# DeltaNet recurrence and gated experts on one core: fused state operations, router columns in the first up product, two products on VectorE

## What is computed

```python
x = x + conv(ln_c(x))                  # conv(n) = t + o @ Wo, t the tokens of n
q, k = l2norm(silu(t @ Wq)), l2norm(silu(t @ Wk))      # 12 heads of 16
v, beta = silu(t @ Wv), sigmoid(t @ Wb)
u_t = beta_t * (v_t - S_{t-1}^T k_t)   # per image and head, S is 16 x 16
S_t = S_{t-1} + k_t u_t^T;   o_t = S_t^T q_t
t = t + ffn(ln_t(t))
probs = softmax(n @ router_w); two best of 8, scaled to sum 1 -> dense_g
routed = sum_e dense_g[e] * (silu(n @ w_gate[e]) * (n @ w_up[e])) @ w_down[e]
shared = (silu(n @ ws_gate) * (n @ ws_up)) @ ws_down
alpha = sigmoid(n @ sg_w + sg_b);   ffn = alpha * shared + (1 - alpha) * routed
```

## Time and profile before

| | us |
|---|---|
| median of 3 runs (497.37 to 498.15) | 497.47 |
| the profiled execution | 497.98 |
| its span | 496.2 |
| busy in it: DVE / PE / POOL / ACT | 428.0 / 425.9 / 414.0 / 349.7 |
| mean granted clock of TensorE | 0.934 |

### The profile page before, as it was taken

The page is one execution under the profiler, slowest core; times in us unless marked ns, Lnnn a source line. Parts: engine busy times, 40 slices in busy tenths (PEclk is TensorE's granted clock), DMA queues, the critical chain, the costliest instruction groups (busy, mean ns, idle before and its releaser), DMA issues.

```text
span 496.2 us, 10722 instructions
## 1 busy us (share of the span) xinstructions
PE 425.9 (86%) x2464; PEld 391.3 (79%) x2464; DVE 428.0 (86%) x2546; ACT 349.7 (70%) x1039; POOL 414.0 (83%) x527
## 2 busy tenths in 40 slices
PE   0344276899999999999999999999999989899996
PEld 0233144789999989899898989898988979898996
DVE  2349989999999999999999999999999999997200
ACT  2795445686878787877778686878786848385763
POOL 5288699989899999999999898998999999896341
PEclk9855555999999999999999999999999999999999
DMA  7948373543323222323233332323222323200300
GB/s 203 223 100 159 94 180 100 111 103 111 79 68 88 72 78 74 92 65 102 68 84 87 81 89 78 89 72 83 80 83 74 83 78 86 81 28 0 114 2 16
DMA packets 44752, 44.12 MB, mean 89 GB/s; under 512 B 19920, under 2 KB 36496, under 8 KB 44688
## 3 DMA queue, kind: packets, MB, share of 16 engines
q1 hardware_dynamic: 40944, 40.87, 32.3%
q10 hardware_dynamic: 3744, 2.57, 1.8%
HBM read 37.13 MB, written 6.29 MB: 87 GB/s over the span
## 4 chain that ended last, share of the span: by engine, by line
DVE 73%; PE 11%; SPq 4%; issue 3%; POOL 3%; DMA 3%; ACT 2%; DVEq 0%; ACTq 0%; POOLq 0%
DVE Pr L1301 16%; DVE u L1303 15%; DVE bank L1305 15%; DVE SH L1309 12%; PE bank L427 2%; DMA k_scratch<-khl 2%; DVE st L1041 2%; SPq L249 2%; SPq L214 1%; DVE ss L1116 1%; PE bank L412 1%; DVE mv L1042 1%; DVE otok L1148 1%; DVE loT L1084 1%; PE bank L400 1%
## 5 line engine op out<-in xcount | busy, mean ns | idle before, releaser
L931 POOL TENSOR_TENSOR hid<-sg,ug 128x192 f32<-128x192 f32 x192 | 112.3, 608 | 23.0 <-ACT ug L669 21.4
L886 POOL TENSOR_TENSOR PQ<-SH,QB 128x768 f32<-128x768 f32 x62 | 112.5, 1835 | 5.8 <-DVE SH L1309 5.8
L1301 DVE TENSOR_TENSOR Pr<-SH,bank 128x96 f32<-128x96 f32 x512 | 104.8, 245 | 4.3 <-PE bank L361 3.9
L893 POOL TENSOR_TENSOR PQ<-PQ 128x768 f32<-128x768 f32 (+2 forms) x93 | 103.3, 1111 | 6.0
L1305 DVE TENSOR_TENSOR bank<-bank,u 128x96 f32<-128x96 f32 x512 | 106.5, 252 | 0.0
L427 PE MATMUL bank<-Wd,hidT 128*128 128x192 f32 x576 | 106.4, 326 | 0.0
L1303 DVE TENSOR_REDUCE u<-Pr 128x6 f32<-128x102 f32 x512 | 105.9, 247 | 0.0
L1309 DVE TENSOR_TENSOR SH<-SH,bank 128x96 f32<-128x96 f32 x512 | 103.0, 241 | 0.0
L427 PEld LDWEIGHTS bank<-Wd,hidT 128*128 128x128 f32 x576 | 95.3, 190 | 0.0
L668 ACT ACTIVATE sg<-bank 128x192 f32<-128x192 f32 x192 | 63.0, 328 | 45.0 <-PE bank L404 25.7
L361 PE MATMUL bank<-KR,Sel 128*128 128x384 f32 x128 | 58.3, 460 | 22.0 <-DVE SH L1309 12.5
(11 more groups left out here) (150 smaller groups left out, 836.6 us busy)
## 6 DMA issues: line engine op xcount, KB each, us to landing
QB<-q_scratch SPq DMA_DIRECT2D x64, 384.0 KB
k_scratch<-khl SPq DMA_DIRECT2D x64, 48.0 KB, 1.7
KR<-k_scratch SPq DMA_DIRECT2D x32, 96.0 KB, 2.4
q_scratch<-qn SPq DMA_DIRECT2D x64, 24.0 KB, 1.6
Wd<-in_L_ffn_w_down_dram SPq DMA_DIRECT2D x4, 288.0 KB, 8.0
out_dram<-xT SPq DMA_DIRECT2D x1, 896.0 KB, 5.2
Wlo_unsplit<-in_L_ffn_w_gate_dram ACTq DMA_DIRECT2D x1, 768.0 KB, 5.6
Wlo_unsplit<-in_L_ffn_w_up_dram ACTq DMA_DIRECT2D x1, 768.0 KB, 8.8
```

The source lines that it names most:

```text
L886: tt(PQ[:, at * BR * HP:(at + n) * BR * HP].rearrange("p (i b h) d -> p i b (h d)", i=n, b=BR), SH[:, lo:lo + n].rearrange("p i b h d -> p ...
L893: chained(tt(PQ[:, :, 0:w], PQ[:, :, 0:w], PQ[:, :, w:2 * w], ALU.add))
L931: tt(hid[:, r * H:(r + 1) * H], sg[:, m % RING], ug[:, m % RING], ALU.mult).then_inc(s_hid, 1)
L1301: v = each(lambda br: count(tt(Pr[:, br, i, :, 0:D], prev[:, br], KB[:, br], ALU.mult)), Sb)
```

## The change

1. In chunks 1 to 15, 17 of the 64 operations (`WHOLE`) are issued as one instruction over both halves, 192 columns; chunk 0 stays as it was. 128 instructions become 111.
2. The 9 logit columns, padded to R = 10, stand in front of unit 0's weights, are split like them, and come out of unit 0's five products, now 394 columns. `Fa_logits`, its weights and the two copies to h2T go. The maximum and the exponentials read unit 0's bank and wait for it. The router's weights are loaded in nine transfers instead of four, ahead of the up weights in SP's queue. The projection of q and k (`A_qk`), which uses bank 1 as well, waits for the split instead of the exponentials.
3. Units 2 and 8: ScalarE takes silu only. VectorE multiplies the up half, read from PSUM, by the gate and by silu in one instruction (`Fb_hidden`) in slots 8 and 38.
4. rstd + 1 is made by ScalarE (`A_plus`). The low parts' zeroed rows and the selectors are waited for where they are first used, no longer by TensorE at its start.
5. The written orders of all engines are changed: in the middle chunks TensorE has unit 0 ahead of fill 7, where `Fa_logits` was, and unit 4 behind the next chunk's fill 2; ScalarE has `A_khi` in the next step's beginning instead of the step's end; VectorE's small stages move by one to ten slots, and `Fa_stats` and `Fa_var`, both in slot 31 before, are in slots 32 and 33.

The core of the diff (cut):

```diff
+DVE_UNITS = (2, 8,)
+R = E + 2
...
+WHOLE = frozenset((9, 22, 31, 32, 33, 38, 39, 49, 50, 51, 52, 53, 54, 55, 56, 57, 58))
...
-        Whi0 = sb("Whi0", [C0, UN, 2 * H], F32R)
-        Wlo0, W1 = fixed("Wlo0", [P, UN, 2 * H], F32R), fixed("W1", [P, UN, 2 * H], F32R)
+        Whi0 = sb("Whi0", [C0, R + UN * 2 * H], F32R)
+        Wlo0, W1 = fixed("Wlo0", [P, R + UN * 2 * H], F32R), fixed("W1", [P, R + UN * 2 * H], F32R)
...
+        def hidden_made(f, m):
+
+            on_dve = sum(k <= m for k in DVE_UNITS)
+            return f * len(DVE_UNITS) + on_dve, f * (UN - len(DVE_UNITS)) + m + 1 - on_dve
+
+        def unit_halves(m):
+
+            at = R if m == 0 else 0
+            return bUp[m % 2][:, at:at + H], bUp[m % 2][:, at + H:at + 2 * H]
...
+        def load_router(eng, i, to, lo, hi):
+
+            eng.dma_start(to[:, 0:E], router_w[lo:hi, :]).then_inc(s_wu[i], 16)
+            for at in range(E, R):
+                eng.dma_start(to[:, at:at + 1], sg_w[lo:hi, :]).then_inc(s_wu[i], 16)
...
-                sp.dma_start(Wr0[:, 0:E], router_w[0:C0, :]).then_inc(s_wr, 16)
-                sp.dma_start(Wr1[:, 0:E], router_w[C0:C, :]).then_inc(s_wr, 16)
-                sp.dma_start(Wr0[:, E:E + 1], sg_w[0:C0, :]).then_inc(s_wr, 16)
-                sp.dma_start(Wr1[:, E:E + 1], sg_w[C0:C, :]).then_inc(s_wr, 16)
+                load_router(sp, 0, raw0[:, :], 0, C0)
+                load_router(sp, 1, raw1[0:C1], C0, C)
+                load_router(sp, 1, raw1[C1:P], C0, C)
                 sp.dma_start(sgb[:, :], sg_b.rearrange("(a n) -> a n", a=1).to_broadcast([P, 1])).then_inc(s_wr, 16)
                 load_up(sp, 1, raw1[0:C1], C0, C)
                 load_up(sp, 1, raw1[C1:P], C0, C)
...
                 if later(a, 4):
-                    pe.wait_ge(s_nmx, a - 3)
-                    pe.wait_ge(s_pr, a - 3)
+                    pe.wait_ge(s_h2T, a - 3)
+                    pe.wait_ge(s_split, a - 3)
...
                 if f == 0:
+                    if c == 0:
+                        pe.wait_ge(s_sel, T // 2)
                     pe.wait_ge(s_KR, c * 32 + 32)
...
-            def Fa_logits(f, p):
-                if f == 0:
-                    pe.wait_ge(s_wr, 80)
-                pe.wait_ge(s_h2T, f + 1)
-                pe.wait_ge(s_split, f + 1)
-                project(bFa[:, 0:E + 1], h2T[:, 0:P], h2T[0:C1, P:2 * P], Wr0[:, :], Wr1[:, :]).then_inc(s_lg, 1)
...
                 if n >= 2 or later(f, 1):
-                    pe.wait_ge(s_ug, f * UN + (n - 1))
-                to = bUp[n % 2][:, 0:2 * H]
-                mm(to, hiT[:, p, 0:P], Whi0[:, n], start=True, stop=False)
-                mm(to, hiT[:, p, 0:P], Wlo0[:, n], start=False, stop=False)
-                mm(to, loT[:, p, 0:P], Whi0[:, n], start=False, stop=False)
-                mm(to, hiT[:, p, P:2 * P], W1[:, n], start=False, stop=False)
-                mm(to, loT[:, p, P:2 * P], W1[:, n], start=False, stop=True).then_inc(s_up, 1)
+                    last = f * UN + n - 2
+                    if last % UN in DVE_UNITS:
+                        pe.wait_ge(s_hidv, hidden_made(last // UN, last % UN)[0])
+                    else:
+                        pe.wait_ge(s_ug, last + 1)
+                w = columns(n)
+                to = bUp[n % 2][:, 0:w.stop - w.start]
+                mm(to, hiT[:, p, 0:P], Whi0[:, w], start=True, stop=False)
+                mm(to, hiT[:, p, 0:P], Wlo0[:, w], start=False, stop=False)
+                mm(to, loT[:, p, 0:P], Whi0[:, w], start=False, stop=False)
+                mm(to, hiT[:, p, P:2 * P], W1[:, w], start=False, stop=False)
+                mm(to, loT[:, p, P:2 * P], W1[:, w], start=False, stop=True).then_inc(s_up, 1)
 
...
-                pe.wait_ge(s_hid, f * UN + -(-hi * P // H))
+                on_dve, on_pool = hidden_made(f, -(-hi * P // H) - 1)
+                if on_dve:
+                    pe.wait_ge(s_hidv, on_dve)
+                pe.wait_ge(s_hid, on_pool)
...
-            pe.wait_ge(s_sel, T // 2)
-            pe.wait_ge(s_low0, 2)
...
+            def A_plus(a, p):
+
+                act.wait_ge(s_rs, a + 1)
+                if later(a, 1):
+                    act.wait_ge(s_xh, a)
+                f(rstd_1[:, :], rstd1, ACT.Identity, bias=one[:, 0:1]).then_inc(s_plus, 1)
+
             def A_xh(a, p):
 
+                act.wait_ge(s_plus, a + 1)
                 act.wait_ge(s_nm1, a + 1)
...
-                f(hiT[C1:P, p, P:2 * P], bFa[0:C1, P:2 * P], ACT.Copy)
-                f(h2T[:, 0:P], bFa[:, 0:P], ACT.Copy)
-                f(h2T[0:C1, P:2 * P], bFa[0:C1, P:2 * P], ACT.Copy).then_inc(s_h2T, 1)
+                f(hiT[C1:P, p, P:2 * P], bFa[0:C1, P:2 * P], ACT.Copy).then_inc(s_h2T, 1)
...
-                f(prob[:, 0:E], bFa[:, 0:E], ACT.Exp, bias=negmax[:, 0:1])
-                f(prob[:, E:E + 1], bFa[:, E:E + 1], ACT.Exp, scale=-1.0, bias=neg_sgb[:, 0:1]).then_inc(s_pr, 1)
+                f(prob[:, 0:E], bUp[0][:, 0:E], ACT.Exp, bias=negmax[:, 0:1])
+                f(prob[:, E:E + 1], bUp[0][:, E:E + 1], ACT.Exp, scale=-1.0, bias=neg_sgb[:, 0:1]).then_inc(s_pr, 1)
...
+                if m in DVE_UNITS:
+                    f(sg[:, m % RING], unit_halves(m)[0], ACT.Silu).then_inc(s_ug, 1)
+                    return
...
-                plus = count(ts(rstd_1[:, :], rstd1, 1.0, None, ALU.add))
-                dve.wait_ge(*plus)
...
-                dve.wait_ge(s_lg, q + 1)
-                w["logit"] = count(nc.vector.tensor_copy(logit[:, :], bFa[:, 0:E]))
-                w["max"] = count(nc.vector.tensor_reduce(negmax[:, :], bFa[:, 0:E], X, ALU.max, negate=True))
+                dve.wait_ge(s_up, q * UN + 1)
+                w["logit"] = count(nc.vector.tensor_copy(logit[:, :], bUp[0][:, 0:E]))
+                w["max"] = count(nc.vector.tensor_reduce(negmax[:, :], bUp[0][:, 0:E], X, ALU.max, negate=True))
...
+            def Fb_hidden(q, p, m):
+
+                dve.wait_ge(s_ug, q * UN + (m + 1))
+                dve.wait_ge(s_gate, q + 1)
+                if m >= UN // 2 or later(q, 1):
+                    last = ((m - UN // 2) % UN + 1) * H - 1
+                    g = [lo * P <= last < hi * P for lo, hi in GRP].index(True)
+                    dve.wait_ge(s_ht, q * NG + (g + 1 - (0 if m >= UN // 2 else NG)))
+                r = m % (UN // 2)
+                nc.vector.scalar_tensor_tensor(out=hid[:, r * H:(r + 1) * H], in0=unit_halves(m)[1],
+                                               scalar=gate[:, p, m:m + 1] if m < E else rden[:, p, 1:2],
+                                               in1=sg[:, m % RING], op0=ALU.mult, op1=ALU.mult).then_inc(s_hidv, 1)
...
+                    elif c < NC:
+                        at(8, -2, Fb_hidden, 2)
+                        at(9, 2, A_low)
+                        at(21, 2, A_z)
+                        at(22, -1, Fa_otok)
+                        at(30, 3, A_stats)
+                        at(31, 3, A_var)
+                        at(32, -1, Fa_stats)
+                        at(33, -1, Fa_var)
+                        at(37, -1, Fa_bias)
+                        at(38, -2, Fb_hidden, 8)
+                        at(39, 1, A_vT)
+                        at(44, -1, Fa_split)
                         at(44, 2, A_ss)
...
                         at(51, -1, G_rank, done)
+                        at(52, 3, A_bias)
                         at(53, -1, G_sel, done)
...
-                        def each(fn, waits):
+                        def each(slot, fn, made):
+
                             got = []
-                            for br in range(BR):
-                                if waits[br] is not None:
-                                    dve.wait_ge(*waits[br])
-                                got.append(fn(br))
+                            for lo in range(BR) if c < 1 or slot not in WHOLE else (0,):
+                                hi = lo + 1 if c < 1 or slot not in WHOLE else BR
+                                for need in dict.fromkeys(made[lo:hi]):
+                                    if need is not None:
+                                        dve.wait_ge(*need)
+                                got += [fn(lo, hi)] * (hi - lo)
                             return got
-                        v = each(lambda br: count(tt(Pr[:, br, i, :, 0:D], prev[:, br], KB[:, br], ALU.mult)), Sb)
+                        v = each(slot, lambda lo, hi: count(tt(Pr[:, lo:hi, i, :, 0:D], prev[:, lo:hi], KB[:, lo:hi], ALU.mult)), Sb)
                         others(slot)
-                        v = each(lambda br: count(nc.vector.tensor_reduce(u[:, i % 2, br], Pr[:, br, i], X, ALU.add, negate=True)), v)
+                        v = each(slot + 1, lambda lo, hi: count(nc.vector.tensor_reduce(u[:, i % 2, lo:hi], Pr[:, lo:hi, i], X, ALU.add, negate=True)), v)
                         others(slot + 1)
-                        v = each(lambda br: count(tt(KB[:, br], KB[:, br],
```

(11 more changed lines are left out.)

## The result

| | before | after |
|---|---|---|
| median of 7 runs each, us | 497.46 (496.97 to 498.96) | 503.33 (500.59 to 504.90) |
| the profiled execution, us | 497.98 | 502.34 |
| its span, us | 496.2 | 500.6 |

What follows compares the result with a forecast made beforehand. VectorE was taken to set the pace, TensorE 3% behind. Start +1.5, chunk 1 -0.2, chunks 2 to 12 -4.6, last three -0.7, tail 0 made -4.0 us: 493.5 us, range 489.3 to 496.8.

Steps and rivals of the forecast that it cites:

- Fused operations: VectorE's 17 whole operations: 1.105 us saved, 0.34 given back where cover is short, net -0.77 us a chunk.
- Two products: Gated products of units 2 and 8 on VectorE: 0.325 us each, +0.65 a chunk; GpSimd's and ScalarE's relief earns nothing directly.
- rstd + 1: Moving this operation from VectorE to ScalarE saves 0.18 us a chunk.
- Variance apart: On VectorE, a whole operation between the second layer norm's mean and variance saves 0.12 us a chunk.
- Start: Five more router transfers in SP's queue ahead of the first k: between 0 and +3.2 us, half taken, +1.5.
- Chunk 1: TensorE's clock is granted at 0.52, so unit 0 comes 0.2 us late for the maximum: gives -0.2 us.
- Router in unit 0: Takes 0.61 us of matrix products off TensorE; slot 48's maximum waits unfelt if unit 0 starts within 0.6 us of the split.
- rival (c): Slower: TensorE begins unit 0 too late and VectorE stalls at slot 48's maximum, 503 us; chance 0.08.
- Chunks 2 to 12: Eleven settled chunks at -0.42 us each, -4.6 us in all.
- Last chunks and tail: Chunks 13 to 15 gain 0.7 us despite less cover; the tail stays at 0, bounds -1 and +1.
- Rival (d): Gains and losses cancel: less cover than counted (-0.2 us a chunk), start costs 2, 496.7 to 498 us; chance 0.08.
- pipe rule (e): VectorE's next operation waits for an empty pipe, so fusing saves 37 us, near 457 us; chance 0.01.

Runs made afterwards that it cites:

- one-wait kernel: The kernel after, but a whole operation that follows two halves waits for the second half alone: 499.23 us, 1.0027 of the kernel before.
- experiment 3: The kernel before with the same 17 operations whole and nothing else changed: 507.14 us, 1.0196 of the kernel before.
- experiment 8: The kernel before with operations 31, 49, 50, 51 whole, waiting for the last half alone, next chunk's fill 0 earlier, rstd + 1 on ScalarE: 493.46 us.
- experiment 9: The kernel of experiment 8 with the second variance one operation after its mean and its bias one slot later: 492.55 us.
- 14: The kernel after with the nine router transfers issued a second time, into an unused tile, ahead of the up weights in SP's queue: 506.92 us.
- experiments 12 and 13: Router's part alone: 12 in the kernel before, 501.54 us; 13 in before with six whole operations, rstd + 1 on ScalarE and earlier fills, 497.37 us.
- experiment 5: The kernel before with only the two products on VectorE, behind slots 3 and 34, and one TensorE turn ahead of a fill: 518.37 us.

## Why the prediction was wrong

- **Fused operations** (-0.77 us a chunk): the step that failed, measured -0.27. The direct costs were right (0.35 long, 0.26 to 0.28 to an independent successor, 0.065 saved with cover on both sides). Wrong was the term for what whole operations give back, 0.34 us a chunk (0.04 to 0.056 for each of six with a short neighbour, 0.04 in slot 22): it took a successor to start 0.38 after a whole operation and counted no wait that stands as an instruction. It should have been 0.84. Of the 0.50 that it lacked, 0.18 are the waits for the first of two halves, shown by the one-wait kernel; 0.17 are the pair's waits in front of Pr in slots 32 and 56, read from the trace and not tried; 0.15 stay unplaced, a part of it that successors start 0.39 to 0.40 us after a whole operation (slots 54, 56, 57, 58), not 0.38. Slot 22's own 0.04 was right once the wait was gone (0.04 in slot 21 with one wait); with no cover at all the entry costs 0.18, wait included (experiment 3). My slot model was right for halves (26.02 against 26.12) and was never tried on a whole operation, of which before has none; "trusted to 0.1" did not follow.
- **Two products** (+0.65): 0.66. Right, the pointer's 0.06 too. But that GpSimd's relief "earns nothing directly" holds only with orders to match: moving them alone, with the orders of the other kernel, cost 11 us in the one direction and 20 in the other.
- **rstd + 1** (-0.18): right, 0.385 against 0.636 in its slot less the fused 0.065, and 0.19 in experiment 8. **Variance apart** (-0.12): the same step gave 0.15 in the slots of experiment 9, and 0.25 in after, where the first variance has moved too.
- **A chunk**: -0.27 + 0.66 - 0.19 - 0.25 = -0.05 us, where the traces show -0.04.
- **Start** (+1.5): +0.9, inside its bounds, but not through the path that I gave: the issues were hidden by SP's idle queue, and the first k landed at 30.2 us (26.39 + 3.77), as in before and as I had named for "wrong". Nor does one trace tell 0.9: the eight traces with the old loads start chunk 1 at 58.6 to 60.9 us, the nine with the new ones (14 aside) at 59.1 to 60.9. The dear end was real: nine more issues cost 5.1. **Chunk 1** (-0.2, measured +0.4): VectorE waited 1.51 us for GpSimd's sums ahead of the transpose of o, where before had 0.79; what made GpSimd late wasn't followed.
- **Router in unit 0**: no idle at the maximum in a settled chunk of after, right. That VectorE had 0.6 us in hand depended on the halves in between: rival (c)'s mechanism appears in experiments 12 and 13, while in after, which came out at its 503 us, it plays no part. Right number, wrong cause.
- **Chunks 2 to 12** (-4.6, measured +1.4): besides the fused term, five stalls at every 128th instruction, 1.4 us against 0.4 before; and chunk 2 alone +0.6, partly a Pr that waited 0.31 us for a fill. Why TensorE is late there wasn't tried.
- **Last chunks and tail** (-0.7 and 0, measured +0.9 and +0.7): the products stay while the cover goes (slot 9 fell by 0.28 there, where the same stage's slot 8 of before fell by 0.40), one stall of 0.37 at record 2495 falls into chunk 14, and the first product stalls the last read-out for 0.79 us. I had 0.33 for it and set it against TensorE's logits.
- Rival (d), "less cover than counted", named the mechanism at a quarter of its size. The pipe rule (e) was rightly set aside; the section that I took it from says itself that a next operation that isn't held starts earlier. The Trainium skill also advises against fusing chained operations (VectorE: DVE Perf Modes, Rules for kernel authors), since the pipe is emptied regardless. The result agrees for operations without cover; with cover the trace does not (slot 50: 0.460 in halves, 0.395 whole).

What stays open: the 0.15 us above, whether moving the pair's wait onto the Pr gives back its 0.17, and why the runs of the line of after spread by 3.7 to 5.8 us (the four of 14 by 1.5) where those of the kernel before, 12 to 20 in each comparison, spread by 3.1 to 4.8.

## What to carry to other kernels

Two half instructions in turn hide each other's latency and each other's waits. Before fusing them count, for each, the work that stands ahead of it and behind it and the waits that it would collect; fuse only inside a run of other work, and wait for the last producer alone, as the wait that the instruction itself carries. Read a named releaser against the code's other waits: in experiment 5 it was the wrong engine. And when the bound engine gets faster, check the next engine's order at each handover: here four well-covered fusions, one operation moved off and one fill earlier gave 1.1%, and the further savings of VectorE that were tried went into waits for TensorE.

## Unexpected on the hardware

- Where a wait that stands as an instruction by itself isn't covered by other work, the next instruction of VectorE starts 0.066 us after the start of its record (0.095 when it holds two waits), against 0.035 us after the producer's end for a carried wait. Five of them fewer in each chunk (75 of 2,760 records) saved 0.18 us a chunk, 2.7 of the 4.1 us from 503.3 to 499.2.
- VectorE can stall by 0.13 to 0.37 us at every 128th instruction, in this program at numbers 63 above a multiple of 128, with nothing named; in most places it is hidden, behind halves as well as whole operations. The Trainium skill (Runtime: NRT & Kernel Launch, Instruction fetch mechanics) has code refilled in blocks of 256 instructions, mostly hidden. Here q14, one of the profile's two instruction queues, moved 0.34 MB in 42 packets, 8 KB each, which at 64 bytes (16 KiB for 256, by that section) are 128 instructions. So the blocks fit, at half the size; that q14 carries VectorE's code, and that the stall is a wait for it, no run shows. What is not hidden was worth 1 us of 500.
